# Attention: head weights made behind the sums, one head a unit; returned tokens asked for behind the swaps

## The reference

```python
c_Q = x @ W_DQ.T
q_C = (c_Q @ W_UQ.T).reshape(B, S, H, D_H).transpose(0, 2, 1, 3)
q_R = rope((c_Q @ W_QR.T)..., pos)
c_KV = x @ W_DKV.T
k_C = (c_KV @ W_UK.T)...;  v = (c_KV @ W_UV.T)...
k_R = rope(x @ W_KR.T, pos)            # shared by the heads
scores = clip(q @ k.T, -80, 80), causal
attn = softmax(scores / sqrt(192)) @ v
out = attn.reshape(B, S, H * D_H) @ W_O.T
x = x + attention(xn) + experts(xn)
```

## Time and profile before

| | |
|---|---|
| median of 3 runs | 1367.82 us (1367.79 to 1369.88) |
| the profiled execution | 1369.01 us, of which the span from first to last instruction is 1367.2 |
| mean granted TensorE clock | 0.985 |
| busy | PE 1303.3, DVE 723.8, ACT 661.8, POOL 623.1 us |
| attention, units 1 to 30 | 733.48 to 1339.35 us of the span |

### The profile page before, as it was taken

The page is one execution under the profiler, slowest core; times in us unless marked ns, Lnnn a source line. Parts: engine busy times, 40 slices in busy tenths (PEclk is TensorE's granted clock), DMA queues, the critical chain, the costliest instruction groups (busy, mean ns, idle before and its releaser), DMA issues.

```text
span 1367.2 us, 20572 instructions
## 1 busy us (share of the span) xinstructions
PE 1303.3 (95%) x6233; PEld 1059.3 (77%) x6233; DVE 723.8 (53%) x1349; ACT 661.8 (48%) x1179; POOL 623.1 (46%) x535
## 2 busy tenths in 40 slices
PE   5999999999999999999997998999999999998998
PEld 4788898888888888888875886877768777776886
DVE  6361164322222222222245877777868768687786
ACT  6421243222222222222245775766757767676775
POOL 5125585991230005000014666656757667576453
PEclk9999999999999999999998999999999999999999
DMA  8125553663241224121142132232332432332012
GB/s 274 51 105 213 197 171 110 186 193 100 90 117 58 63 62 146 56 63 63 40 158 80 32 78 44 55 63 53 78 53 47 77 56 52 70 51 49 17 47 93
DMA packets 82167, 123.34 MB, mean 90 GB/s; under 512 B 20176, under 2 KB 28496, under 8 KB 82064
## 3 DMA queue, kind: packets, MB, share of 16 engines
q1 hardware_dynamic: 51216, 60.62, 15.6%
q0 software_dynamic: 11312, 27.23, 9.2%
q10 hardware_dynamic: 19536, 34.17, 7.6%
HBM read 74.41 MB, written 39.05 MB: 83 GB/s over the span
## 4 chain that ended last, share of the span: by engine, by line
PE 87%; DVE 4%; issue 3%; POOL 2%; DMA 1%; ACT 1%; SPq 1%; ACTq 0%; DVEq 0%; POOLq 0%
PE bank L49 80%; PE bank L1481 2%; DVE acc L1339 2%; PE bank L1423 2%; PE bank L1566 2%; DVE store_b L1238 1%; DMA rot_sin<-sum_b 1%; SPq L450 1%; DVE store_b L1312 1%; DMA rows_b<-in_x 1%; ACT store_b L850 1%; POOL rot_sin L581 0%; POOL sum_b L617 0%; PE bank L1409 0%; POOL rot L586 0%
## 5 line engine op out<-in xcount | busy, mean ns | idle before, releaser
L49 PE MATMUL bank<-store_b,store_a 128*128 128x512 f32 (+1 forms) x1536 | 331.6, 369 | 1.7 <-issue 1.2
L49 PE MATMUL bank<-slots,x_turned 128*128 x1296 | 317.5, 394 | 0.3 <-DVE x_turned L950 0.3
L49 PEld LDWEIGHTS bank<-store_b,store_a 128*128 128x128 f32 x1536 | 265.5, 195 | 64.7 <-issue 12.7
L49 PEld LDWEIGHTS bank<-slots,x_turned 128*128 128x128 f32 x1296 | 239.2, 188 | 48.3 <-issue 0.7
L972 DVE TENSOR_TENSOR hid_t<-bank,hid_t 128x512 fp32r<-128x512 f32 x70 | 48.4, 691 | 343.8 <-ACT hid_t L682 343.8
L49 PE MATMUL bank<-slots,hid_t 128*128 (+1 forms) x840 | 208.4, 397 | 0.0
L49 PE MATMUL bank<-store_b 128*128 128x512 f32 x768 | 180.0, 389 | 2.3 <-ACT bank L861 2.3
L49 PEld LDWEIGHTS bank<-slots,hid_t 128*128 128x128 f32 x840 | 153.7, 188 | 30.8
L49 PEld LDWEIGHTS bank<-store_b 128*128 128x128 f32 x768 | 143.9, 188 | 33.4 <-issue 3.6
L1312 DVE TENSOR_TENSOR store_b<-p_store,store_b 128x512 fp32r<-128x512 f32 x128 | 131.8, 1032 | 29.3 <-ACT store_b L850 29.3
L553 POOL CAST slots<-staging 128x512 f32 (+1 forms) x84 | 51.6, 614 | 188.0 <-PE bank L49 171.8
(11 more groups left out here) (201 smaller groups left out, 1792.5 us busy)
## 6 DMA issues: line engine op xcount, KB each, us to landing
staging<-in_w SPq DMA_DIRECT2D x56, 256.0 KB, 2.7
sorted_y<-y_store ACTq DMA_DIRECT2D x54, 256.0 KB, 2.0
rows<-sorted_x ACTq DMA_DIRECT2D x51, 260.0 KB, 2.7
rot_sin<-sum_b SPq DMA_DIRECT2D x128, 64.0 KB, 2.0
staging<-in_wg SPq DMA_DIRECT2D x28, 256.0 KB, 2.8
shared_y<-y_store ACTq DMA_DIRECT2D x16, 256.0 KB, 2.0
raw<-in_wot SPq DMA_DIRECT2D x16, 256.0 KB, 2.9
acc<-in_x SPq DMA_DIRECT2D x16, 256.0 KB, 5.4
```

The costliest lines, as they stand in the source:

```text
L49: made = pe.matmul(out, a, b, start=first and n == 0, stop=last and n == len(pairs) - 1, skip_group_check=onto)
```

## The change

1. Head weights of unit u are made behind `attend(u)` (behind the sums row) and not ahead of it: in PE's list, in the ring's order (the sums row takes its bank before the head's two), in ScalarE's list (behind L916) and VectorE's (behind L1396).
2. One head a unit for every pair: pair 1's two heads are made in units 1 and 2 and no longer both in unit 0. Their raw weights are loaded where they were.
3. The 16 loads of `acc` are no longer issued ahead of the units. The four of sequence u are issued in unit u (0 to 3), behind `swap_halves(u + 1)`.

```diff
         def heads_of(u):
 
             p, b = units[u]
-            if p + 1 == PAIRS:
-                return ()
-            return {0: (0, 1)}.get(b, ()) if p == 0 else {1: (0,), 2: (1,)}.get(b, ())
+            return {1: (0,), 2: (1,)}.get(b, ()) if p + 1 < PAIRS else ()
...
+            ring.take("sums", u)
             for h in heads_of(u):
                 ring.take("head", p + 1, h, 0)
                 ring.take("head", p + 1, h, 1)
-            ring.take("sums", u)
...
             swap_halves(0)
-            for h in heads_of(0):
+            for h in range(2):
                 head_weights(1, h)
             sp.wait_ge(on["y_done"], NBK)
-            for b in range(NB):
-                for t in range(b * TB, (b + 1) * TB):
-                    sp.dma_start(acc[:, t, :], x_t[:, t, :]).then_inc(on[f"x_back{b}"], 16)
             for u, (p, b) in enumerate(units):
                 if u + 1 < NU:
                     swap_halves(u + 1)
+                if u < NB:
+                    for t in range(u * TB, (u + 1) * TB):
+                        sp.dma_start(acc[:, t, :], x_t[:, t, :]).then_inc(on[f"x_back{u}"], 16)
...
-                for h in heads_of(u) if u else ():
+                for h in heads_of(u) if p else ():
                     head_weights(p + 1, h)
...
(ScalarE)
-                for h in heads_of(u):
-                    head_weights(p + 1, h, 0)
-                    head_weights(p + 1, h, 1)
                 for n in range(2):
                     if u:
                         act.wait_ge(on["out_done"], TB * u)
...
                     on["rows_made"], 1)
+                for h in heads_of(u):
+                    head_weights(p + 1, h, 0)
+                    head_weights(p + 1, h, 1)
...
(VectorE)
-                for h in heads_of(u):
-                    head_weights(p + 1, h, 0)
-                    head_weights(p + 1, h, 1)
                 for n in range(2):
                     dve.wait_ge(on["o_high"], 2 * u + n + 1)
...
+                for h in heads_of(u):
+                    head_weights(p + 1, h, 0)
+                    head_weights(p + 1, h, 1)
...
(TensorE)
                 if u:
                     output(u - 1)
+                attend(u)
                 for h in heads_of(u):
                     head_weights(p + 1, h, 0)
                     head_weights(p + 1, h, 1)
-                attend(u)
```

## The result

The changed kernel takes 1314.87 us (median of 4, 1313.76 to 1315.45) against 1368.33 us beside it: a ratio of 0.9607, interval 0.959 to 0.9623, so 53.5 us or 3.9% faster. The forecast was 1315.0.

A forecast was written before the change was run, and what follows sets the result against it. TensorE bounds the kernel, with head products stalled on query subtractions, slow clock behind. 49.2 - 2.6 + 6.8 + 0.6 - 1.2 = 52.8 us saved from the 1367.82 median gives 1315.0 us, range 1308 to 1329.

The forecast's parts named there:

- a: Heads behind the sums: waits and slow clock go in twelve head units, products stay at 1.2 us each, 14.4 us.
- b: Head evictions on ScalarE and VectorE delay the next unit's clips: 2.0 us lost over twelve units, bounds nothing to 5.0.
- c: First pair's two heads move from unit 0 to units 1 and 2: 2.6 us lost, 0.2 of it lateness.
- d: Unit 0, swap issued before loads: unit 1 starts at 726.7, 6.8 us saved, plus 0.6 of slow clock.
- e: Four acc loads behind the swaps of units 0 to 3: 0.3 us a unit, 1.2 lost, bounds 0 and 3.8.
- 19.1 to 20: Sign of being right: head units take this many us at clock 1.00.
- A first clip later than +3.3: Sign of being wrong: VectorE's first clip starts more than 3.3 us into a unit.
- The slow clock: Lower TensorE clock after unit 0's remaining wait: 1.6 us against 2.2 before, bounds nothing to 3.2.
- The late chain: Rival: in every head unit lateness costs PE in full (5.0 us) and a head 1.55: 1322.9 us, chance 0.14.
- unit 0's stall: Rival: unit 0's sums still wait, swap packets travelling with the loads: 1319.0, or 1320.6 with second slow stretch, chance 0.09.
- the moved wait: Rival: the sums row waits for the first query subtraction, 0.9 us in each of fourteen units: 1337 us, chance 0.05.
- the head's subtractions in the scores: Slower case: next unit's last two score products wait for head banks; 4.3 us a unit gives 1375, chance 0.03.

The follow-up runs named there:

- x5: Changed kernel with each head product of pairs 1 to 7 issued twice into the same bank: 1329.53 us against 1365.9 for the kernel before.
- x11: The changed kernel itself, run again on another call as a measure for further variants: 1314.88 us, ratio 0.9632 to the kernel before.
- x4: Changed kernel with the acc loads all ahead of the units again: 1322.9 us against 1366.22 for the kernel before.
- x2: Kernel before with only the order changed, heads behind the sums row on every engine and in the ring: 1322.42 us against 1366.22.
- x1: Kernel before with only the acc loads issued by sequence behind the swaps: 1361.84 us against 1366.22.
- x7: Changed kernel with both additions of expert rows moved into the next unit, ahead of its third clip and third probability subtraction: 1320.64 us against 1365.9 before.

## Why the prediction was right

Point by point, forecast against the trace:

| step | forecast | measured |
|---|---|---|
| a, b: units 5 to 30 | 49.2 saved | 47.4 (532.00 to 484.56) |
| a head's products | 1.2 | 1.04 in units 10 and 14, 1.10 for a second copy (x5) |
| b: lateness in units 5 to 30 | 2.0 | about 5.5, in x11 3.6 |
| c, d, e: units 1 to 4 | 3.2 lost | 0.3 lost (73.87 to 74.17) |
| d: start of unit 1 | 726.7 | 727.08 |
| e: loads behind the swaps | 1.2 | nothing in units 2 and 3 (x4) |
| sum | 52.8 | 53.5 |

The mechanism held, and the range holds the result with room to spare. That the forecast is within 0.2 us of the result is luck: lateness cost 3.5 us more than forecast and unit 1 started 0.4 later, the heads were 1.8 cheaper and units 1 to 4 2.9, and these cancel to 0.7. Single executions differ by more than that too.

**Heads behind the sums (a).** Right in place and size: the waits for the query subtractions are gone, with x2 as the one-part proof. A head was mis-sized by 0.15, which in twelve units gave 1.8 us. Head units took 18.68 to 19.92 us, most of them 18.95 to 19.2, where I had named 19.1 to 20.

**What waits for the evictions (b).** The mechanism was right, the size not. The excess of units 5 to 30 over 17.9 each is 19.2; twelve heads at 1.05 make 12.6, the units that were long before (12, 20, 24, 28) 1.1, and 5.5 remain where I had 2.0, outside the bounds of 0 to 5.0 that I gave this term. A first clip later than +3.3, which I had named as a sign of being wrong, came twice, at +3.81 in unit 6 and +3.36 in unit 18. I had taken 0.9 of VectorE's head work as nearly covered by 1.2 us of head products; with the real 1.05, of which about 0.4 falls only in the next unit's first scores (unit 7: 18.27 without a head of its own), the first clip of unit 6 comes later than 3.0: at +3.31 to 3.32 in the other three profiles of this order (x2, x4, x11), and at +3.81 here, behind the late landing in unit 5. The rest is lateness on SyncE and the queues: the last of unit 9's swap issues took 1.97 us where 0.6 is usual, and PE waited 1.21 us at the end of that unit. x2 and x4 have 1.22 and 1.18 there and 484.8 and 484.7 for units 5 to 30, x11 has 0.62 and 482.67, so it isn't a single accident; what makes these issues long stays open.

**Unit 0 (d).** The time came out as reckoned, from the swap and GpSimd's chain: issue at 714.32 (714.4), multiplication at 718.28 (718.5), end of L622 at 726.56 (726.0). But the wait that I had left over, 3 to 4 us for GpSimd, isn't there: PE waits 2.3 us for VectorE's L1310 instead, and the rest of `attend` is drawn out. The unit's end is GpSimd's, whose chain from L579 to the end of L622 takes 8.28 us, not the 7.5 that I took: before it took 7.12, with VectorE idle, and now L612, L615 and L617 take 1.74, 1.54 and 1.06 us where their like took 1.26, 1.26 and 0.72. So working at once with VectorE costs unit 0 about 1.1 us. The slow clock, which I had put into unit 1 for 1.6 us, came at 0.90 into unit 0, where PE had to wait anyway, and in x1's profile not at all. Units 1 to 4 were mis-sized by 2.9 us in all: 1.6 for this clock, 1.2 for the loads, 0.3 for the heads' price, less 0.2 for lateness.

**Loads behind swaps (e).** Units 1 to 3 multiply at +8.82 to 8.83, beside 8.74 in unit 4 and 8.80 in units 2 and 3 of x4, without the loads. Transfers issued behind the swap didn't hold it up, and the 1.2 us that I gave this term measured nothing. The Trainium skill ("DMA: Bandwidth & Descriptors", Queues, rings and completion order) has descriptors of a ring consumed in order; the trace agrees with it here. Unit 5's late landing, which I had set against it, is there in the first profile of the changed kernel (multiplication 9.96 into the unit), but not in x2, x4 and x11, which have 8.70 to 8.73 with the same transfers behind it.

**The rivals.** The late chain holds in part (3.6 to 5.5 us of lateness, no 1.55 a head); unit 0's stall went (x1, x4); the moved wait didn't come, but in the changed kernel the first query bank is free only 0.3 to 1.3 us before the sums row, and VectorE's lateness in x7 used that up; nothing waited for the head's subtractions in the scores.

## What to carry to other kernels

A product that needs a bank late in the ring and nothing else may be what stalls the matrix engine: put the work that depends on fewest late results first, and write the ring in the same order. Count a wait of the matrix engine with what its clock loses behind it: here 30.7 us of waits cost about 13 us more. And on an engine's list the idle gaps are not equal: an addition that fills a gap beside a busy GpSimd, or ahead of something a bank waits for, may cost more than it gives.

## What the runs showed of the hardware

A VectorE instruction with both operands in SBUF (128x512) takes 0.68 to 0.69 us while GpSimd is idle; in unit 0 three of them took 5.00 instead of 1.90 us, and the addition of x7 took 1.77. L1236, with one operand in PSUM, stayed at 0.67 to 0.69. The Trainium skill ("GPSIMD Engine Reference", Specifications) names contention with VectorE instructions of two SBUF inputs; the trace agrees.

The order of starting decides which engine pays. In attention the changed kernel has 90 such instructions of VectorE (L1310, L1385) that meet a GpSimd TENSOR_TENSOR. 58 started at least 0.02 us behind GpSimd's, and each ended 0.54 to 0.62 us behind the end of GpSimd's, however long that still ran. In the other 32 the two started within 0.02 us of each other or VectorE was first; these took VectorE 0.67 to 0.69 us, and GpSimd's instruction took up to 0.6 us longer than its like alone. So in this trace the engine that comes second waits until the other is through, which is why the same VectorE instruction can cost 0.7 us in one gap and 1.8 in the next.

Filling the matrix engine's waits with products that nobody reads made the kernel before faster by 0.65%.
